# Neighbour counts of a four-layer GNN: edges sorted by destination chunk on the chip, one chunk of destinations counted per tile

## The reference, cut to what matters

```python
def rgcn_gate_layer(x, row, col, edge_type, basis, att, gate_w, root, bias):
    w = jnp.einsum('rb,bio->rio', att, basis)          # 2 x 512 x 512 out of 30 bases
    x_j = x[col]
    msgs = []
    for r in range(2):
        gate = jax.nn.sigmoid(x_j @ gate_w[r, :, 0])
        msgs.append(gate[:, None] * x_j @ w[r])
    msg = jnp.where((edge_type == 0)[:, None], msgs[0], msgs[1])
    return jax.ops.segment_sum(msg, row, num_segments=625) + x @ root + bias

h = jnp.maximum(_layernorm(x), 0.0)
x = x + _L0_gnn_ref(h, ...)     # the layer above, relu, the layer again with other weights
x = x + _L1_gnn_ref(relu(ln(x)), ...)   # GCN: uses counts of both types and degrees
x = x + _L2_gnn_ref(relu(ln(x)), ...)   # edge MLP: uses edges sorted by dst, with attributes
x = x + _L3_gnn_ref(relu(ln(x)), ...)   # edge layer: uses edges sorted by src
```

## Time and profile before

| | before |
|---|---|
| median of three runs (lowest to highest) | 1295.84 us (1293.26 to 1300.98) |
| profiled execution: time, span | 1297.59 us, 1295.8 us |
| TensorE busy | 1214.3 us, 94% |
| VectorE busy | 795.6 us, 61% |
| ScalarE busy | 556.7 us, 43% |
| GpSimd busy | 510.5 us, 39% |
| moved by DMA | 175.86 MB, of which 89.34 MB + 11.02 MB before 560 us |
| mean granted TensorE clock | 0.973 |

### The profile page before, as it was taken

The page is one execution under the profiler, slowest core; times in us unless marked ns, Lnnn a source line. Parts: engine busy times, 40 slices in busy tenths (PEclk is TensorE's granted clock), DMA queues, the critical chain, the costliest instruction groups (busy, mean ns, idle before and its releaser), DMA issues. The chain is left out here.

```text
span 1295.8 us, 15266 instructions
## 1 busy us (share of the span) xinstructions
PE 1214.3 (94%) x4908; PEld 646.6 (50%) x4908; DVE 795.6 (61%) x1576; ACT 556.7 (43%) x975; POOL 510.5 (39%) x442
## 2 busy tenths in 40 slices
PE   7898899599999999899999999999999979899995
PEld 3433433244544444555555555555555546445552
DVE  5764564667322323267778777777778756846663
ACT  1021211210110211357777777777777733225552
POOL 1111111253242000277766666666666100047661
PEclk9999899799999999889999999999999989999998
DMA  8699686555400201496544444444444020036662
GB/s 342 230 342 362 236 316 247 180 185 166 175 15 8 95 1 43 117 221 154 109 94 94 95 97 92 96 91 98 92 96 82 1 68 1 17 123 201 185 183 79
DMA packets 59444, 175.86 MB, mean 136 GB/s; under 512 B 12485, under 2 KB 13029, under 8 KB 52584
## 3 DMA queue, kind: packets, MB, share of 16 engines
q0 software_dynamic: 32496, 76.65, 25.0%
q1 hardware_dynamic: 26872, 98.23, 20.9%
HBM read 160.32 MB, written 14.52 MB: 135 GB/s over the span
## 5 line engine op out<-in xcount | busy, mean ns | idle before, releaser
L1184 PE MATMUL PS<-w,hidT 128*128 128x512 f32 x696 | 315.1, 595 | 0.0
L542 POOL DMA_INDIRECT rec_scratch<-rec_src,slot_row x84 | 99.4, 1184 | 287.6 <-DMA rec_scratch<-rec_src,slot_row 234.1
L1184 PEld LDWEIGHTS PS<-w,hidT 128*128 128x128 f32 x696 | 132.3, 191 | 134.0 <-issue 126.7
L1007 POOL DMA_INDIRECT pair_sum<-table_i,counts_rec x87 | 87.4, 1004 | 219.1 <-POOLq L63 130.7
L1015 POOL DMA_INDIRECT pair_sum<-table_j,counts_rec x87 | 147.6, 1697 | 30.7 <-issue 26.2
L1119 ACT ACTIVATE grow<-PS 128x512 f32<-128x512 f32 x174 | 104.0, 598 | 119.1 <-PE PS L1167 83.9
L1280 POOL DMA_INDIRECT u_space<-table_j,rec x87 | 82.3, 946 | 130.8 <-DMA table_j<-agg_rows 94.1
L269 PE MATMUL PS<-is_src,is_dst 128*128 128x512 bf16 x420 | 111.6, 397 | 20.4 <-DVE is_src L575 19.3
L1124 ACT ACTIVATE grow<-grow,two 128x512 f32<-128x512 f32 x174 | 124.8, 717 | 5.0 <-DVE grow L1065 4.9
L1065 DVE SCALAR_TENSOR_TENSOR grow<-grow 128x512 f32<-128x512 f32 x174 | 120.6, 693 | 6.0
L317 PE MATMUL PS<-w_rel,hT 128*128 128x512 f32 x240 | 107.6, 605 | 13.6 <-DMA w_rel<-w_scratch 11.9
(11 more groups left out here) (216 smaller groups left out, 1795.2 us busy)
## 6 DMA issues: line engine op xcount, KB each, us to landing
ring<-basis_rows SPq DMA_DIRECT2D x48, 1024.0 KB, 7.4
ring<-basis_low SPq DMA_DIRECT2D x30, 512.0 KB, 4.6
w_scratch<-stage SPq DMA_DIRECT2D x96, 32.0 KB
rec_scratch<-ring POOLq DMA_DIRECT2D x2, 1496.0 KB, 14.8
counts_rec<-rec_scratch SPq DMA_DIRECT2D x1, 2992.0 KB, 10.7
rec_scratch<-rec_src,slot_row POOLq DMA_INDIRECT x168, 3.5
root<-L_gnn_root SPq DMA_DIRECT2D x2, 1024.0 KB, 7.8
w_rel<-w_scratch SPq DMA_DIRECT2D x1, 2048.0 KB
```

Of the source, the lines that this page charges most:

```text
L542: nc.gpsimd.indirect_dma_start(out=rec3_dram, out_offset=bass.IndirectOffsetOnAxis(ap=slot_row[:, 1, t:t + 1], axis=0), in_=rec, in_offset ...
L1007: nc.gpsimd.indirect_dma_start(out=pair_sum[:, t % GOT3, :], out_offset=None, in_=tables[0][0], in_offset=bass.IndirectOffsetOnAxis(ap=idx ...
L1184: m = nc.tensor.matmul(o, hidT[:, t % 2, k * P:(k + 1) * P], w2[:, k, :], start=False, stop=(k == KT - 1), skip_group_check=True)
```

## The change

The sort of the edges is computed first, with nothing of the counting ahead of it. It is then used twice: for the scatters, as before, and for the counting. The tiles are sorted on the chip with one-hot products: for each of 84 tiles VectorE writes four small one-hots (`move_hots`), and one product of 264 columns (`sort`) puts destination, type and source of every edge in its sorted slot in PSUM bank 6. `read_moved` takes them out. Then NS = 87 sorted tiles are counted, each for one chunk of destinations: two one-hots (128 and 640 wide, `count_hots`) and two products into a bank that a register picks (`count`). The chunk numbers are packed eight to a word (`pack_chunks`). The banks are cleared by a product with zeros (`clear`).

Around it the orders of all engines are written anew: 6 mixes ahead of the sort loop, 12 in it, 22 in the count loop, 8 between the Y0 products; `w_rel[0]` is read back at load 37; slot 3 of the basis ring and then slot 2 are given to Y0 results. No `sum2` and no low piece comes before the end of all basis pieces; `records()` moves from tile 20 of the count loop to tile 66 of the sort loop, and `later_records(1)` to behind the last `unpack`.

```diff
-            RING1, RING2, COLS1, COLS2, STAGE, HOT = 4, 4, 32, 16, 6, 4
+            RING1, RING2, COLS1, COLS2, STAGE, HOT = 4, 4, 32, 16, 6, 6
-            MIX_AFTER = [6, 7, 8, 9, 11, 13] + [24 + 10 * j // 7 for j in range(COLS1 + COLS2 - 6)]
-            T0_AFTER, G0_AFTER, LOW_WITH, LOW_AFTER_W1 = 52, 57, range(25, 43, 2), 14
-            SUM2_AT = range(48, ET, 2)
-            SUM2_BEFORE_H1 = (18, 6, 6, 6, 6)
+            MIX_FIRST, MIX_SORT, MIX_COUNT = 6, range(2, ET, 7), range(1, NS, 4)
+            T0_AT, G0_AT, R0_SORT, R0_COUNT = range(12, 37, 6), 44, (52, 66), (18, 40, 62)
+            LATE_MIX = {1: (COUNT_MIXED,), 2: (COUNT_MIXED + 1,), ... 7: (COUNT_MIXED + 7,)}
+            W1_BEFORE = 37
+            SUM2_BEFORE_H1 = (38, 6, 6, 6, 4)
 # TensorE
-                def count(t):
-                    ...five products of 512 columns, five of 128, into banks 0 to 6
+                def sort(e):
+                    pe.wait_ge(sem("one_hot"), 4 * e + 4)
+                    nc.tensor.matmul(PS[:, MOVE_BANK, 0:3 * SC], is_slot[:, e % HOT, :], is_src[:, e % HOT, 0:3 * SC],
+                                     start=(e == 0), stop=(e == ET - 1), skip_group_check=True).then_inc(sem("hot_used"), 1)
+                def count(t, c):
+                    pe.wait_ge(sem("one_hot"), 4 * ET + 2 * t + 2)
+                    nc.tensor.matmul(PS[:, bass.ds(c, 1), :]..., is_slot[:, t % HOT, :], is_src[:, t % HOT, 0:512], ...)
+                    nc.tensor.matmul(tails[:, bass.ds(c, 1), :]..., is_slot[:, t % HOT, :], is_src[:, t % HOT, 512:NP],
+                                     ...).then_inc(sem("hot_used"), 1)
+                for t in range(NS):
+                    if t % PART == 0:
+                        clear(t // PART)
+                    if t % 8 == 0:
+                        word = pe.value_load(words[0:1, t // 8:t // 8 + 1], min_val=0, max_val=8**8 - 1)
+                    count(t, (word >> 3 * (t % 8)) & 7)
 # SyncE
-                for n in range(RING1):
-                    load(n)
+                load(0)
                 sp.dma_start(slot_of_col[:], ...)
                 sp.dma_start(earlier[:], ...); sp.dma_start(earlier_tile[0:ET, :], ...)
+                load(1)
+                sp.dma_start(x_rows[:, 0:NT - 1, :], ...)
+                load(2)
+                sp.dma_start(ident[:], ...); sp.dma_start(gate_cols[:], ...)
+                load(3)
                 for n in range(RING1, COLS1 + COLS2):
                     load(n)
+                    if n == W1_BEFORE:
+                        ...wait for the stores of sub-layer 1, read w_rel[0] back
                     if n % 2:
                         store(n - 5)
-                    if n in LOW_WITH:
-                        load_low(LOW_WITH.index(n))
                 for n in (COLS1 + COLS2 - 4, COLS1 + COLS2 - 2):
                     store(n)
                 sp.dma_start(rows_in[:], ...)
-                for b in range(len(LOW_WITH), LOW_AFTER_W1):
+                for b in range(RING2):
                     load_low(b)
                 ...wait for all stores, read w_rel[1] back
-                for b in range(LOW_AFTER_W1, NB):
+                for b in range(RING2, NB):
                     load_low(b)
 # VectorE
+                def move_hots(e):
+                    if e >= HOT:
+                        dve.wait_ge(sem("hot_used"), e - HOT + 1)
+                    nc.vector.tensor_scalar(is_slot[:, e % HOT, :], node_of_col[:, 0:P], slot[:, 1, e:e + 1], None,
                                             ALU.is_equal).then_inc(sem("one_hot"), 1)
+                    for j, value in enumerate((values[:, 0, :], values[:, 1, :], place[:, 0, :])):
+                        nc.vector.tensor_scalar(is_src[:, e % HOT, SC * j:SC * (j + 1)], node_of_col[:, 0:SC], slot_tile[:, 1, e:e + 1],
+                                                value[:, e:e + 1], ALU.is_equal, ALU.mult).then_inc(sem("one_hot"), 1)
+                def count_hots(t):
+                    dve.wait_ge(sem("hot_used"), ET + t - HOT + 1)
+                    nc.vector.tensor_scalar(is_slot[:, t % HOT, :], node_of_col[:, 0:P], by_chunk[:, 0, t:t + 1], None, ALU.is_equal)...
+                    nc.vector.tensor_scalar(is_src[:, t % HOT, :], node_of_col[:], by_chunk[:, 2, t:t + 1], by_chunk[:, 3, t:t + 1],
                                             ALU.is_equal, ALU.mult).then_inc(sem("one_hot"), 1)
+                groups()
+                ...mixer
+                tile_counts()
+                places()
+                slots(1)
+                norm_stats_dve(dve, 0, x_rows)
+                chunks(1)
+                pack_chunks()
+                slots(0)
+                norm_rows_dve(dve, 0, x_rows, h_rows)
+                for e in range(ET):
+                    move_hots(e)
+                    if e == 60:
+                        gate("G0", 1, slice(0, 2 * NT))
+                    if e == 66:
+                        records()
+                read_moved()
+                for t in range(NS):
+                    count_hots(t)
+                    for c in range(NT):
+                        if t == PART + 5 + 2 * c:
+                            unpack(0, c)
+                        if t == 2 * PART + 5 + 2 * c:
+                            unpack(1, c)
+                chunks(0)
                 for c in range(NT):
                     unpack(2, c)
+                later_records(1)
                 ...bias, then for each chunk: SUM2_BEFORE_H1[c] times sum2, h1(c)
                 later_records(2)
                 ...gates of sub-layer 2
 # ScalarE: the same order as TensorE's; between the Y0 copies the late mixes' copies
```

More of the change, by code:

```diff
@@ L243, in gnn_stack @@
+            assert COUNT_MIXED + 8 == NCOLS and COLS1 < W1_BEFORE and sum(SUM2_BEFORE_H1) <= 2 * NB
+            assert max(n for n in range(NCOLS) if slot_of[n] == 3) < COUNT_MIXED
+            assert max(n for n in range(NCOLS) if slot_of[n] == 2) <= COUNT_MIXED + 5
             side = {}
@@ new lines, in clear @@
+                def clear(g):
+                    if g:
+                        pe.wait_ge(sem("packing"), NT * g)
+                        pe.wait_ge(sem("packed"), NT * g)
+                    else:
+                        pe.wait_ge(sem("zeros"), 1)
+                        pe.wait_ge(sem("rank_read"), 2)
+                        pe.wait_ge(sem("by_chunk"), 5)
+                    for bank in range(7):
+                        nc.tensor.matmul(PS[:, bank, 0:512 if bank < 6 else TAIL], none[:, 0:P], none[:, 0:512 if bank < 6 else TAIL],
+                                         start=True, stop=False, skip_group_check=True)
@@ new lines, in _ @@
+                mix(0, solo(piece(0)))
+                tile_sums()
+                mix(1, solo(piece(1)))
+                pe.wait_ge(sem("per_tile"), 1)
+                pe.wait_ge(sem("tri_in"), 32)
+                rank(1)
+                mix(2, solo(piece(2)))
+                mix(3, solo(piece(3)))
+                pe.wait_ge(sem("rank_read"), 1)
+                rank(0)
+                for n in range(4, MIX_FIRST):
+                    mix(n, solo(piece(n)))
+                for e in range(ET):
+                    sort(e)
+                    if e in MIX_SORT:
+                        n = MIX_FIRST + MIX_SORT.index(e)
+                        mix(n, solo(piece(n)))
+                    if e in T0_AT:
+                        c = T0_AT.index(e)
@@ L361, in _ @@
                         pe.wait_ge(sem("root_in"), 16)
+                        product(c, root, solo(("R0", c))).then_inc(sem("side_mm"), 1)
+                pe.wait_ge(sem("words"), 1)
+                for t in range(NS):
[4 more added lines that the diff above has]
+                    count(t, (word >> 3 * (t % 8)) & 7)
+                    if t in MIX_COUNT:
+                        n = SORT_MIXED + MIX_COUNT.index(t)
+                        mix(n, solo(piece(n)))
+                    if t in R0_COUNT:
+                        c = len(R0_SORT) + R0_COUNT.index(t)
@@ new lines, in _ @@
+                groups()
+                dve.wait_ge(sem("att_in"), 48)
+                for l in range(2):
+                    nc.vector.memset(mixer[l][:], 0.0).then_inc(sem("mixer_zero"), 1)
+                dve.wait_ge(sem("mixer_zero"), 2)
+                for l in range(2):
+                    for r in range(2):
+                        nc.vector.tensor_scalar(mixer[l][:, 4 * r:4 * r + 4], quarter[:], att_col[l][:, r:r + 1], None,
+                                                ALU.mult).then_inc(sem("mixer"), 1)
```

276 lines of the change are left out of this document (131 added, 145 removed).

## The result

The changed kernel takes 1362.02 us (median of 4 runs, 1359.02 to 1368.47) against 1294.86 for the kernel before in the same comparison: 1.0521 times as long, 95% interval 1.0478 to 1.0565, or 67 us by the medians. I had forecast slower by 17 us. The direction and the place were right, the size was not, and the time lies above the range of 1274 to 1336 us.

What follows compares the result with a forecast made beforehand. Bound by two chains meeting at 332 to 333 us: counting through h1, and the first 56 scatters. The scatters end 24 us later, less 4 head start, rounded to +17: 1314.6 profiled, 1313 us median; range 1274 to 1336.

Steps and rivals of the forecast that it cites:

- A sorting tile: Sort loop on VectorE: four small one-hots per tile, 0.16 + 3 x 0.21 = 0.80 us, bounds 0.52 and 1.20.
- The line of the scatter's period: GpSimd's scatters: period 2.35 us + 0.0103 us per GB/s of DMA traffic, fitted to three windows of the earlier profile.
- TensorE's head start of one pair of products: TensorE makes the first Y1 pair (7.1 us) while waiting for `later_records(2)`, which gives back 4 of 24 us.
- Rival 4: Count loop: choosing the bank in a register holds TensorE up, 1.3 us a counting tile, +30, 1326 us; chance 0.12.
- Rivals 1 to 3: 1: VectorE's own chain decides, 1272 us (0.17); 2: small one-hots cheap, 1290 us (0.07); 3: prices cancel, 1296 us (0.18).
- Rival 1: Scatters keep up, VectorE's own chain decides, if 56 scatters take under 3.6 us each: 1272 us; chance 0.17.
- 240 to 319, 17 scatters at 4.6 us, the last 11 at 3.1, `later_records(2)` at 357: Second 28 scatters, priced by DMA traffic at 220 GB/s, then quieter; with a 4.5 us reload, 24 us later than before.
- S: Moment when `later_records(1)` passes, after the first 28 scatters and their reload; forecast at 240 us.
- the set-up: VectorE's steps before sorting (groups, `slots` twice, statistics, chunk table): done and sort loop starting at 40 us.
- my rounding from 20 to 17: Net delay 24 - 4 = 20 us, taken as +17 because the period line was read under a deeper queue.
- The last h1: End of VectorE's bias, 60 `sum2` of 1.20 us (72 us) and five h1 of 0.69: forecast at 319 us.
- The count loop: 87 tiles of 0.52 us plus unpacks and part changes on VectorE, 75 us, TensorE hidden: from 108 to 185 us.

Runs made afterwards that it cites:

- x1: Changed kernel, each `sum2` replaced by a product with one SBUF input, 1023 columns, without accumulation: 1334.21 us, ratio 1.0256 to the kernel before.
- x3: Changed kernel, complete, each `sum2` waiting for the one just before it instead of the one before that: 1347.01 us, ratio 1.0363 to the kernel before.
- y4: Kernel before, without sorted counting, `records()` at count tile 50 instead of 20 and `later_records(1)` behind the last unpack: 1328.03 us, ratio 1.0225.
- x4: Changed kernel, `later_records(2)` moved on VectorE behind sub-layer 2's gates and the inverse roots: 1310.69 us, ratio 1.0073 to the kernel before.
- y3: Changed kernel, `records()` and `later_records(1)` earlier, `later_records(2)` behind the inverse roots, `rows_in` and low pieces loaded from basis piece 38: 1293.41 us, ratio 0.9965.
- x2: Changed kernel, each `sum2` replaced by two dense one-input products of 1024 columns, without accumulation: 1354.22 us, ratio 1.0407 to the kernel before.

## Why the prediction was wrong

**What held.** The chain of scatters is what decides, and `later_records(2)` is where it does: forecast a wait over 25 us, measured 52.23, TensorE idle 45.7, and all behind it shifted alike. A sorting tile takes VectorE 98.81 - 98.01 = 0.80 us, as worked out. The line of the scatter's period came within 5% for the first 28 scatters (132.1 us at 254 GB/s are 4.72 us each, the line gives 4.97). For the next 28, without the block, it was 18% too high in x1 (111 us at 227 GB/s are 3.96, the line gives 4.69) and right to 1% in x3 (123.6 us at 198 GB/s are 4.41, the line gives 4.39). TensorE's head start of one pair of products was there. Rival 4 (the bank in a register) didn't occur: the clean counting tiles lie 209.46 - 208.94 = 0.52 us apart on VectorE, the estimate for its one-hots alone. Rivals 1 to 3 needed an earlier or a cheaper chain and didn't occur. (Rival 1's bound of 3.6 us a scatter is 209 / 56 = 3.7; nothing else rests on it.)

**The step that failed: 240 to 319, 17 scatters at 4.6 us, the last 11 at 3.1, `later_records(2)` at 357.** From S to that column I had 357 - 240 = 117 us; it took 396.94 - 253.39 = 143.6. The term priced a scatter by the traffic alone, and the hold by `sum2` at nothing of its own. Four held scatters make up 44.9 us of it, by what they last beyond 0.96 us. Taking the block away gave back less, since the scatters that then ran met more traffic: in x1 the stretch took 371.07 - 255.44 = 115.6 us, with `sum2` faster than before, and in x3 383.23 - 254.04 = 129.2, with `sum2` slower. Against y4, whose block is 13 us, the changed kernel loses 30. So the block is 14 to 28 us by removal, and the 26.6 us too many lie in that range; how they split between the block and traffic that lasted longer than I had it is not settled closer than this.

I had the sign of it in the trace of before: in the window of the earlier trace rows from 204 to 327 us, GpSimd is busy 41.43 us for 28 scatters, 1.48 each, and 29.34 for 28 in the window before it. Most of the surplus is one scatter of 10.66 us, under a burst of 18 `sum2`, and it ends 0.83 us behind that burst. I averaged it into the period as if it were traffic. Since the change makes one burst out of two, its price is not an average but the rest of the burst: 36 x 1.20 = 43 us, less what had passed by then.

**The second miss: S.** Forecast 240, measured 253.39. The first scatter left at 113.5 instead of 94. Half of this is the set-up, 50.2 instead of 40: `x_rows` came so late that VectorE waited 5.59 us, and the second `slots` needed a product that TensorE made behind a mix whose basis piece it had waited 13.37 us for. I had taken the set-up as VectorE's own chain. The rest is VectorE waiting for TensorE inside the sorting loop, 8.0 us in two waits, 6.92 of them at the gates; I had priced this loop with TensorE hidden. So 50.2 + 67 x 0.80 + 8.0 = 111.8, and `records()` stands at 112.2. Of these 19.5 us the scatters made up 6, having less traffic to meet. The two misses are 13.4 + 26.6 = 40 us, the difference of 357 and 397. Of the time, 61.4 us between the profiled executions against 17 forecast, the rest is my rounding from 20 to 17 and a head start that gave back 63.8 - 61.4 = 2.4 us instead of 4.

**The third, not on the deciding path here but next to it.** The last h1 came at 344.03, forecast 319. The bias waited 12.70 us for `rows_in`, since SyncE issues it and the low pieces at 261 us, behind the last mix's load, and `sum2` began at 269.3, not 243. The count loop had ended at 217 instead of 185. This is what x4 leaves of the loss, and what y3 takes away.

**What would have been enough.** With the block priced by the row of 10.66 us as "until 0.83 us behind the burst", a scatter caught 10 us into a burst of 36 x 1.20 = 43 costs 33, or 28 more than an ordinary one; the forecast would have been 1313 + 28 = 1341 us by this estimate, and the late start would have been left over. The Trainium skill has rules that bear on it (SBUF — State Buffer). "Who interferes with whom" says that a VectorE instruction with two SBUF inputs contends with a GpSimd instruction that reads SBUF, and infers for `tensor_tensor` that it doesn't stall a DMA issued by GpSimd, because writing descriptors needs the other interface. These scatters take their row numbers from `slot_row` in SBUF, so the first sentence can cover them and agrees with the held scatters. The inference would have made me expect none, and the trace speaks against it: 35.00 us under `scalar_tensor_tensor`, and 4.04 us instead of 0.96 under the one `tensor_tensor` of 3.47 us. "SBUF: two separate sides" says that a fast one-input form, its example is an fp32 `tensor_copy`, keeps GpSimd from writing descriptors. x2's `tensor_scalar` stream, fast by its 0.66 us apiece, agrees: 14 scatters waited for the end of an instruction and one for the end of a run. No run here tells reading the row numbers apart from writing the descriptors.

## What to carry to other kernels

Look at the longest single instruction of a GpSimd DMA queue, not at its mean: a mean of 1.5 us was 27 scatters of 1.1 us and one held until a burst on VectorE ended. Work that comes off the busiest engine is worth what the next chain leaves free, so find the next wait first, and what the new order puts ahead of it. Where a slow chain of small transfers must run beside VectorE's accumulations, keep the wait for it behind the work that everything else needs (51 us here by moving one line), start it as early as its inputs allow, and break up long runs (15 us here by one changed wait).

## What the runs showed of the hardware

- A scatter waits for the end of a VectorE instruction. In the eleven traces 86 scatters that begin under `sum2`, or under what x1 and x2 put in its place, last over 1.0 us, and all of them end 0.83 or 0.84 us behind the end of a VectorE instruction. That holds with one SBUF input as with two.
- In a back-to-back run it can miss one boundary after the other. Under two-input `scalar_tensor_tensor` (eight kernels) 24 of 58 were held over at least two more instructions, 23 of these to the end of the run, up to 36.40 us. Under one input it was 1 of 15 in x2 and 0 of 7 in x1.
- A short gap lets it in: 0 of 16 were held on in x3, with 0.10 us behind each instruction, and in y3 a single pause of 0.05 us set one free.
- What tells the held ones apart stays open: at 275.04, 4.4 us into the burst of 36, one passed in 1.28 us, while those 3.5 us into a burst of six were held.
- A mix at the lower level of TensorE's clock takes 1.94 us instead of 1.06, and both occur between the sorting products, where the granted clock was 0.71 from 56 to 112 us; each thing that stands on TensorE between two sorting products then costs VectorE's ring of one-hots more.
